# Which queue fetches the rows of the last edge tiles of a graph layer, and where the message scales are computed

## The reference

```python
def _mlp(h, W, b, gamma, beta):
    h = jax.nn.relu(h @ W + b)
    mu = jnp.mean(h, axis=0)
    var = jnp.mean(jnp.square(h - mu), axis=0)
    return gamma * (h - mu) * jax.lax.rsqrt(var + EPS) + beta
h = jnp.maximum(_layernorm(x, axis=-1), 0.0)
node_feat = _mlp(h, W_node, b_node, g_node, beta_node)
edge_feat = _mlp(edge_attr, W_edge, b_edge, g_edge, beta_edge)
message = jnp.concatenate([h[src], h[dst], edge_feat], axis=1)
message = _mlp(message, W_msg, b_msg, g_msg, beta_msg)
agg = jax.ops.segment_sum(message, dst, num_segments=6250)
out = x + agg + node_feat
```

## Time and profile before

| | us |
|---|---|
| median of 3 runs (lowest, highest) | 996.18 (995.70, 998.44) |
| the profiled execution | 996.0 |
| span of the profile, first to last instruction | 994.1 |

### The profile page before, as it was taken

How to read it: one execution, slowest core, us unless ns; L and a number is a source line. 1 busy time by engine, 2 the same in 40 slices (tenths; PEclk the granted TensorE clock), 3 DMA queues, 4 the chain that set the end, 5 groups by cost and what they waited for, 6 DMA issues and landing times.

```text
span 994.1 us, 22967 instructions
## 1 busy us (share of the span) xinstructions
PE 759.2 (76%) x4820; PEld 605.1 (61%) x4820; DVE 531.6 (53%) x1422; ACT 369.7 (37%) x624; POOL 732.0 (74%) x778
## 2 busy tenths in 40 slices
PE   2735786676369999999999997777776776677687
PEld 2604562222158888888888886666665665566573
DVE  8577878878735555555555554343433333333345
ACT  3733696666323333333333332222222222222230
POOL 6777777777777777777777777777777777777770
PEclk9856797556569999999999999998999788887899
DMA  9575533333533333333333332332332322222223
GB/s 295 128 286 151 129 74 80 74 76 80 149 70 73 73 76 73 72 75 73 74 75 73 75 73 65 64 65 63 66 67 63 66 64 58 61 58 61 58 57 103
DMA packets 95826, 87.43 MB, mean 88 GB/s; under 512 B 67365, under 2 KB 71989, under 8 KB 95624
## 3 DMA queue, kind: packets, MB, share of 16 engines
q0 software_dynamic: 24768, 38.09, 17.8%
q1 hardware_dynamic: 68992, 47.18, 17.7%
q10 hardware_dynamic: 1992, 1.50, 0.6%
HBM read 68.80 MB, written 14.54 MB: 84 GB/s over the span
## 4 chain that ended last, share of the span: by engine, by line
SPq 39%; issue 19%; POOL 12%; PE 11%; DMA 10%; ACT 4%; DVE 4%; ACTq 1%; DVEq 0%; POOLq 0%
SPq L496 20%; POOL ring L528 12%; SPq L446 6%; SPq L489 5%; DMA ring<-p_table,src_idx 4%; DMA xs<-x_stack 4%; PE pc L750 3%; SPq L432 2%; SPq L321 2%; SPq L487 2%; PE pd L870 2%; DMA big_a<-zeros 2%; PE pc L859 1%; SPq L473 1%; ACT r_sb L646 1%
## 5 line engine op out<-in xcount | busy, mean ns | idle before, releaser
L528 POOL DMA_INDIRECT ring<-p_table,src_idx x726 | 686.2, 945 | 221.4 <-issue 202.8
L870 PE MATMUL pd<-hm 128*97 128x193 f32 x1564 | 316.9, 348 | 18.2 <-ACT hm L694 18.2
L870 PEld LDWEIGHTS pd<-hm 128*97 128x97 f32 x1564 | 258.8, 176 | 28.6 <-ACT hm L694 20.9
L859 PE MATMUL pc<-w3q,r_sb 128*128 128x96 f32 x1564 | 223.6, 288 | 37.9 <-ACT r_sb L684 36.1
L684 ACT ACTIVATE r_sb<-pa 128x512 f32<-128x512 f32 x196 | 116.8, 596 | 307.0 <-issue 133.5
L859 PEld LDWEIGHTS pc<-w3q,r_sb 128*128 128x128 f32 x1564 | 197.6, 198 | 43.9 <-issue 24.7
L1126 DVE TENSOR_TENSOR pc<-pc,ring 128x384 f32<-128x384 f32 x194 | 109.5, 564 | 157.3 <-POOLq L557 94.3
L1110 DVE TENSOR_SCALAR hm<-pb 128x384 f32<-128x384 f32 x196 | 109.1, 557 | 134.2 <-PE pb L844 85.8
L694 ACT ACTIVATE hm<-pc 128x384 f32<-128x384 f32 x196 | 96.2, 491 | 189.8 <-DVE pc L1126 182.0
L1047 DVE BATCH_NORM_STATS2 edge_st<-r_sb 96x512 f32 (+1 forms) x196 | 121.6, 675 | 35.8 <-ACT r_sb L646 34.4
L838 PE MATMUL pa<-xs,we_stack 128*128 128x512 bf16 x196 | 79.4, 405 | 64.6 <-DMA xs<-x_stack 64.0
(11 more groups left out here) (116 smaller groups left out, 419.2 us busy)
## 6 DMA issues: line engine op xcount, KB each, us to landing
w3q<-q_table SPq DMA_DIRECT2D x782, 11.2 KB
ring<-p_table,src_idx POOLq DMA_INDIRECT x726
ln_buf<-p_table ACTq DMA_DIRECT2D x704, 0.4 KB
xs<-x_stack SPq DMA_DIRECT2D x98, 72.0 KB
x_stack<-ring SPq DMA_DIRECT2D x6, 980.0 KB, 5.6
xs<-x_stack SPq DMA_DIRECT2D x98, 60.0 KB, 1.9
ln_buf<-p_table SPq DMA_DIRECT2D x320, 0.4 KB
ring<-in_x_nodes SPq DMA_DIRECT2D x5, 480.0 KB, 9.2
```

The costliest lines, as they stand in the source:

```text
L528: nc.gpsimd.indirect_dma_start(out=ring[:, tile * C:(tile + 1) * C], out_offset=None, in_=table, in_offset=bass.IndirectOffsetOnAxis(ap=id ...
L859: last = nc.tensor.matmul(pc[:, j % 2, t * C:(t + 1) * C], r_sb[:, j % 2, t * TILE:(t + 1) * TILE], w3q[:, j, t, :], start=True, stop=True)
L870: last = nc.tensor.matmul(pd[0:M1, j % 2, 0:HW], hm[:, j, t, WIN:HW], hm[:, j, t, :], start=(t == 0), stop=(t == n - 1))
```

## The change

- Two more tiles, the last two of group 189, are brought by register-addressed transfers: ten tiles (758 to 767) in place of eight. Group 189's addition on DVE is split in two, one half from `ring`, one from `far`.
- The 32 rows of the last tile are brought by SP with 32 register-addressed transfers of their own, two per group in groups 150 to 165 (`LAST_AT`), with four register loads of 8 indices, and one transfer that zeroes the tile's other 96 partitions.
- GpSimd issues 723 gathers from `p_table` in place of 726.
- Of the 1280 rows ACT now does partitions 0 to 86, 870 rows in place of 704, three per group up to group 110 and then 540 over 75 groups. SP does 410 rows in place of 320: 102 of them in the first phase (6 per iteration in place of 9), and 308 in place of 167 in the main loop, over groups 110 to 184. An index load is for 10 rows in place of 8.
- The message's mean, variance and the request for the root (`message_scales`) come between the last addition to `gram` and the last addition to `agg`, with one instruction fewer, and the vector after the root is made with one instruction fewer.

```diff
-FAR_T = len(FAR) * TPG
-FAR_BY_ACT = 88
+FAR_T0, FAR_T = FAR[0] * TPG - 2, len(FAR) * TPG + 2
+FAR_BY_ACT = 87
 BACKLOG = 110
-FAR_P1 = 9 * (P1_LOOPS - P1_PEELED - 1)
+FAR_P1 = 6 * (P1_LOOPS - P1_PEELED - 1)
+LAST_AT = 150
...
         src_idx = sb("src_idx", [P, NTILES], i32)
+        last_idx = sb("last_idx", [1, LAST_ROWS], i32)
...
+        def far_group(t):
+
+            return (FAR_T0 + t) // TPG - FAR[0] + 1
+
+        def pool_tiles(g):
+
+            return [t for t in range(g * TPG, g * TPG + tiles(0, g)) if
+                    t != NTILES - TPG + LAST_TILES - 1 and not FAR_T0 <= t < FAR_T0 + FAR_T]
...
             def due(h):
-                late = (rows - first - early * BACKLOG) * (h - BACKLOG) // (FAR[0] - BODY - BACKLOG)
+                late = (rows - first - early * BACKLOG) * (h - BACKLOG) // (FAR[0] - BODY - 1 - BACKLOG)
                 return first + (early * h if h <= BACKLOG else early * BACKLOG + late)
 
-            return range(due(g), due(g + 1)) if g < FAR[0] - BODY else ()
+            return range(due(g), due(g + 1)) if g < FAR[0] - BODY - 1 else ()
...
-            at_tile = FAR[0] * TPG
             _, at_node = nc.values_load_multi_w_load_instructions(
-                src_idx[p:p + 1, at_tile:at_tile + FAR_T], [engine], min_val=0, max_val=N,
...
-                    if n // 9 == i - P1_PEELED - 1:
+                    if n // 6 == i - P1_PEELED - 1:
...
+            sp.wait_ge(last_idx_in, 16)
             outside = sp.value_load(flag[0:1, 0:1], min_val=0, max_val=2 * P)
             with sp.If(outside < 1):
+                last_at = ((NG - 1) % RING * TPG + LAST_TILES - 1) * C
+
+                def load_last(n):
+
+                    nonlocal last_nodes
+                    if n == 0:
+                        sp.wait_ge(pre_added, NG - RING)
+                        sp.dma_start(ring[LAST_ROWS:P, last_at:last_at + C], zeros[LAST_ROWS:P, 0:C]).then_inc(last_in, 16)
+                    if n % 8 == 0:
+                        _, last_nodes = nc.values_load_multi_w_load_instructions(
+                            last_idx[0:1, n:n + 8], [mybir.EngineType.SP], min_val=0, max_val=N,
+                            skip_runtime_bounds_check_because="a node of an edge, below N by the kind of input")
+                    for p in range(n, n + 2):
+                        sp.dma_start(ring[p:p + 1, last_at:last_at + C],
+                                     p_table[bass.ds(last_nodes[p % 8], 1), :]).then_inc(last_in, 16)
+
+                last_nodes = None
                 for g in range(NG):
                     i, j = at(0, g)
                     if g % 2 == 0:
@@ -497,11 +527,13 @@
                                      q_table[bass.ds(at_node[g % 2 * TPG + t], TWIN), :]).then_inc(q_in[j], 16)
                     for n in far_part(g, FAR_P1, (P - FAR_BY_ACT) * FAR_T, 0):
                         load_far(n)
+                    if LAST_AT <= g < LAST_AT + LAST_ROWS // 2:
+                        load_last(2 * (g - LAST_AT))
                     if j == BODY - 1:
                         load_res(i)
...
-                for t in range(tiles(0, g)):
-                    tile = g * TPG + t
+                for tile in pool_tiles(g):
...
-                by_pool = [g for g in range(RAW, NG) if g not in FAR]
+                by_pool = [g for g in range(RAW, NG) if pool_tiles(g)]
+                landed = [0] * 4
...
-                        pool.wait_ge(gather_done[m % 4], 64 * (m // 4) + 16 * tiles(0, by_pool[m]))
+                        landed[m % 4] += 16 * len(pool_tiles(by_pool[m]))
+                        pool.wait_ge(gather_done[m % 4], landed[m % 4])
                         pool.sem_inc(gathered, 1)
...
+            act.dma_start(last_idx[:, :], src_last).then_inc(last_idx_in, 16)
...
-                    for n in far_part(g, 0, FAR_BY_ACT * FAR_T, 2):
+                    for n in far_part(g, 0, FAR_BY_ACT * FAR_T, 3):
                         load_far(n)
...
+            def message_scales():
+
+                V.tensor_tensor(diag[:, :], gram[0:C, 0:C], ident[0:C, 0:C], ALU.mult)
+                link(V.tensor_scalar(sc[:, 0:1], gram[0:C, C:M1], -1.0 / E, None, ALU.mult))
+                V.tensor_tensor(sc[:, 2:3], sc[:, 0:1], sc[:, 0:1], ALU.mult)
+                link(V.tensor_reduce(sc[:, 1:2], diag[:, :], AX, ALU.add))
+                link(V.scalar_tensor_tensor(sc[:, 3:4], sc[:, 1:2], 1.0 / E, sc[:, 2:3], ALU.mult, ALU.subtract))
+                V.tensor_scalar(sc[:, 11:12], sc[:, 3:4], 0.0, EPS, ALU.max, ALU.add).then_inc(sqrt_asked, 1)
...
                     if isinstance(g, int) and g in FAR:
-                        dve.wait_ge(far_in[g - FAR[0]], 16 * P * TPG)
-                        rows = far[:, (g - FAR[0]) * (TPG * C):(g - FAR[0] + 1) * (TPG * C)]
+                        t = g * TPG - FAR_T0
+                        dve.wait_ge(far_in[far_group(t)], 16 * P * TPG)
+                        rows = far[:, t * C:t * C + n]
+                    elif isinstance(g, int) and g == FAR[0] - 1:
+                        n = FAR_T0 % TPG * C
+                        dve.wait_ge(gathered, g + 1)
+                        V.tensor_tensor(pc[:, j % 2, 0:n], pc[:, j % 2, 0:n],
+                                        ring[:, g % RING * (TPG * C):g % RING * (TPG * C) + n], ALU.add)
+                        dve.wait_ge(far_in[0], 16 * P * (TPG - FAR_T0 % TPG))
+                        V.tensor_tensor(pc[:, j % 2, n:TPG * C], pc[:, j % 2, n:TPG * C], far[:, 0:TPG * C - n],
+                                        ALU.add).then_inc(pre_added, 1)
+                        return
                     else:
                         dve.wait_ge(gathered, g + 1 - far_before(g))
+                        if isinstance(g, int) and g == NG - 1:
+                            dve.wait_ge(last_in, 16 * (LAST_ROWS + 1))
                         rows = ring[:, bass.ds((g % RING) * (TPG * C), n)]
                     V.tensor_tensor(pc[:, j % 2, 0:n], pc[:, j % 2, 0:n], rows, ALU.add).then_inc(pre_added, 1)
...
                     V.tensor_tensor(gram[:, :], gram[:, :], pd[0:M1, j % 2, WIN:HW], ALU.add).then_inc(gram_added, 1)
+                    if isinstance(g, int) and g == NG - 1:
+                        dve.wait_ge(gram_added, NG)
+                        message_scales()
                     wait(dve, win_added, g)
                     V.tensor_tensor(agg[:, bass.ds(base, WIN)], agg[:, bass.ds(base, WIN)], pd[0:M1, j % 2, 0:WIN],
                                     ALU.add).then_inc(win_added, 1)
...
-            link(V.tensor_tensor(diag[:, :], gram[0:C, 0:C], ident[0:C, 0:C], ALU.mult))
-            link(V.tensor_reduce(sc[:, 1:2], diag[:, :], AX, ALU.add))
-            V.tensor_scalar(sc[:, 0:1], gram[0:C, C:M1], 1.0 / E, None, ALU.mult)
-            link(V.tensor_scalar(sc[:, 1:2], sc[:, 1:2], 1.0 / E, None, ALU.mult))
-            link(V.tensor_tensor(sc[:, 2:3], sc[:, 0:1], sc[:, 0:1], ALU.mult))
-            link(V.tensor_tensor(sc[:, 3:4], sc[:, 1:2], sc[:, 2:3], ALU.subtract))
-            V.tensor_scalar(sc[:, 11:12], sc[:, 3:4], 0.0, EPS, ALU.max, ALU.add).then_inc(sqrt_asked, 1)
             dve.wait_ge(sqrt_done, 2)
             link(V.reciprocal(sc[:, 12:13], sc[:, 12:13]))
             link(V.tensor_tensor(sc[:, 8:9], sc[:, 12:13], vec[:, G_MSG:G_MSG + 1], ALU.mult))
             V.tensor_scalar(fold[:, 0:C], ident[0:C, 0:C], sc[:, 8:9], None, ALU.mult)
-            link(V.tensor_tensor(sc[:, 9:10], sc[:, 0:1], sc[:, 8:9], ALU.mult))
-            V.tensor_tensor(fold[:, C:M1], vec[:, BT_MSG:BT_MSG + 1], sc[:, 9:10],
-                            ALU.subtract).then_inc(fold_ready, 1)
+            V.scalar_tensor_tensor(fold[:, C:M1], sc[:, 8:9], sc[:, 0:1], vec[:, BT_MSG:BT_MSG + 1], ALU.mult,
+                                   ALU.add).then_inc(fold_ready, 1)
...
+        "src_last": src[E - LAST_ROWS:E][None, :],
```

18 lines of the change are left out of this document (12 added, 6 removed).

## The result

The changed kernel takes 1106.03 us (median; 1102.08 to 1108.06), the one before 996.57 us on the same chip (995.7 to 998.44). The ratio is 1.1095, 95% interval 1.108 to 1.111. The forecast was 1023 (1006 to 1042). It went the way that was forecast, but the loss is 109.5 us where 27 were forecast. The profiled execution has a span of 1103.5 us and took 1105.47.

The account below looks back on a forecast made before the run. SP's queue was taken to set the pace to the end: group 110's addition at 590, plus 412 to the last at 1002, plus 20.0 less 0.6, span 1021.4, plus 1.9 outside it: 1023 us, range 1006 to 1042.

Parts of the forecast that it names:

- The step that failed: SP's queue: a far row with its share of the index load costs 0.50 us, bounds 0.45 and 0.54.
- ACT, "2 us, bounds 0 and 15": ACT's queue before group 110: the third row per group is mostly hidden, charged 2 us for all 110 groups.
- rival 2: ACT falls behind too, its third row per group not hidden before group 110: about 1041, up to 1060 us; chance 9%.
- SP sets the pace from start to end: Main loop: SP's 85 us more work exceeds its cover, about 35 us uncovered, so POOL is waited for no more.
- The cover of 36.5 us: SP's queue waits 31.4 + 5.1 us from 745 to 965, which could absorb added work.
- The main loop of 412 us from group 110 on: SP's time from group 110's addition to the last: 240.4 for groups, 154 for far rows, 17.6 for last-tile rows.
- First phase, -13 us, bounds -8 and -18: First phase: 17 iterations fall from 6.5 to 5.7 us with DVE as bound, so the main loop starts 13 us earlier.
- Three gathers fewer, -3.75: POOL: three gathers fewer at 1.25 us each save 3.75 us, if POOL still sets the end.
- The scales, -0.6: Kernel's end: message scales start 0.15 us earlier with fewer instructions before the root, -0.6 us, bounds -0.2 and -0.9.
- The tail, 20.0 - 0.6: From the last addition to the end: 20.0 us as before, less 0.6 for the scales.
- Rival 1: POOL still sets the end, faster by three gathers and the scales: 991.7 us; chance 7%.

Follow-up runs that it names:

- experiment 3: The change with index loads of 8 from column 760 in place of 10 from 758, on both queues: 1006.96 us, ratio 1.0106.
- experiment 4: The change with ACT's index load of 8 from column 760, SP's still of 10 from 758: 1075.28 us, ratio 1.0793.
- experiment 7: The kernel before with only the last tile's 32 rows by SP and the earlier scales, far tiles left at eight: 994.57 us, ratio 0.9983.
- experiment 8: The change with index loads of 8 from column 760, without PE's twelve unread products ahead of the last two window sums: 1006.29 us, ratio 1.0098.

## Why the prediction was wrong, point by point

- **The step that failed** is "With a load of 0.86 for ten rows in place of eight I take 0.50 a row, and as bounds 0.45 and 0.54". It took a load's price as nearly independent of the number, from loads that all had eight indices and started at column 760. The change starts at 758, and the load costs 2.41 us: one step for each of the ten indices, where the eight from column 760 cost two. On SP a far row with a tenth of its load is 0.43 + 0.24 = 0.67, outside both bounds. The rows of before show one form only, eight from column 760, so the load was an operation not shown and had to be bounded by itself. The two bounds came from two readings of rows that all held this same load; they bounded the row, not the load.
- What it is worth: experiment 3 has the change with loads of 0.80 and takes 1006.96. The long loads make the other 99 us: 68 on SP (experiment 4 against 3), 31 on ACT (the change against experiment 4). In spans SP's are 1072.3 - 1007.0 = 65.3 (the profiled execution of experiment 3, 1009.16 us, is the slowest of its four), of which 12.3 lie ahead of the first addition; for the other 53 the 30 loads of SP's main loop at 2.40 - 0.80 = 1.6 more give 48.
- **ACT, "2 us, bounds 0 and 15"**: 31 us, in the way that rival 2 (1041 to 1060, 9%) named, "where the index load falls ahead of the relu", but not by the third row that the rival charged. ACT has 33 loads between 276 and 625; PE waited for the relu 31 times there, 45.0 us, and SP for PE 31 times. With a load of eight the same third row costs nothing: 316 us for 111 additions in experiment 3. So the verdict on the row was right, and the load wasn't asked about.
- **SP sets the pace from start to end**: right in experiment 3. In the change it holds after group 110 only; up to there ACT set it. SP's waits after 625 are 0.4 us in all, and DVE's waits for gathers fell from 94.3 to 6.6.
- **The cover of 36.5 us**: right in kind. It was all used, and the kernel before with the last tile's rows (experiment 7) still had 22.4 us of the wait for line 893, where it was 31.4.
- **The main loop of 412 us from group 110 on**: 407.5 in experiment 3, so the terms of that sum hold together, to 4.5 us.
- **First phase, -13 us, bounds -8 and -18**: mis-sized, hidden in the result under the long loads (the first addition came 8.3 us earlier). In experiment 3 it is 284.84 - 262.79 = 22. The step took DVE's busy time, 5.4 us an iteration, as its floor and added start-up for 5.7. The 5.4 adds two rows that overlap in part (line 1090 is busy for 0.40 us, and the next operation starts 0.32 us after it) and divides 139 operations by 17 iterations, which is more than eight each. From 145 to 230 us line 1090, once an iteration, ran 16 times in experiment 3, 5.3 us each, already below it. In the change it ran 14 times. With 5.3 the 17 iterations save 17 x (6.5 - 5.3) = 20. Experiment 3:

```profile
145.00:230.00 85.00, 6.39 (x16) 0.90 0.36 87
```

- **Three gathers fewer, -3.75**: the last gather moved from 970.72 to 966.90, as forecast (967), and was worth nothing, also as forecast.
- **The scales, -0.6**: 0.62 in experiment 7; the root 1.36 us after the last addition to `gram` starts, 2.11 before. **The tail, 20.0 - 0.6**: it is 1103.5 - 1082.0 = 21.5, not 19.4. The missed part is the idle products: without them it is 1004.9 - 985.5 = 19.4 in experiment 8. Before, they ran while everybody waited for the last gathers, and the forecast had taken exactly that wait away.
- Set against experiment 3, the forecast's span of 1021.4 is 14.4 us above the measured 1007.0: 9.2 by the first addition (272 and 262.79), 3.0 by the first 110 groups (318 and 315.0, 2 of it ACT's), 4.5 by the rest of the main loop, less 2.3 by the tail (19.4 and 21.7). The load of ten made 99 us, and the other way. With the load as priced the measured 1006.96 would have lain 1 us inside the low end of the range. The change would still have been slower, but by 11 us where 27 were forecast.
- **Rival 1** (991.7): it needed a far row at 0.39 us of SP's time. Giving ten partitions to ACT relieves SP in another way. With loads of twelve POOL then sets the end, as the rival says, at 994.15 and 992.88 us on a chip where the kernel before takes 997.5. With loads of sixteen the 992.82 us is near its number too, but ACT's queue is what is late. Its mechanism is possible, only not for this change.

## What to carry to other kernels

When an edit changes the operands of an instruction whose price was read from the trace (its count, its first column), the old price is a price of the old form: bound it by one read per element (here 0.21 us each, on top of 0.34), and look whether the new start is still a multiple of four. Here loading six indices that nobody needs, so that the load starts at a multiple of four, was worth 78 us. And a price paid once in ten rows isn't an average where the queue that pays it has an engine's next instruction behind it: on ACT the 2.5 us stood in one piece ahead of a relu, 33 times before group 110, and PE waited for that relu 31 times.
